# Transformer block on one core: Gelu's output and w2 split into f16 parts for the MLP's second product

## The reference

```
mod = swish(c) @ w_mod + b_mod                      # shifts, scales, gates
xn  = ln(x) * (1 + sc_msa) + sh_msa
q, k, v = heads(xn @ w_qkv + b_qkv);  q = ln(q, g_q);  k = ln(k, g_k)
x   = x + g_msa * (softmax(q k^T / 3) v @ w_proj + b_proj)
xn2 = ln(x) * (1 + sc_mlp) + sh_mlp
h   = gelu_tanh(xn2 @ w1 + b1)
out = x + g_mlp * (h @ w2 + b2)
```

## Time and profile before

| | us |
|---|---|
| median of 3 runs (190.43 to 191.2) | 190.98 |
| the profiled execution | 189.51 |
| its span | 187.7 |
| TensorE (PE) busy | 168.4 |
| VectorE (DVE) busy | 126.3 |
| ScalarE (ACT) busy | 107.4 |
| GpSimd (POOL) busy | 62.8 |

### The profile page before, as it was taken

One profiled execution on the slowest core, in us unless ns is written; L12 is line 12 of the kernel. 1 busy time (PEld: TensorE's weight loads), 2 busy tenths in 40 slices (PEclk: granted clock), 3 DMA queues, 4 the chain that ended last, 5 costly groups with the idle time before them and its releaser, 6 DMA issues.

```text
span 187.7 us, 4037 instructions
## 1 busy us (share of the span) xinstructions
PE 168.4 (90%) x1579; PEld 98.8 (53%) x1579; DVE 126.3 (67%) x317; ACT 107.4 (57%) x148; POOL 62.8 (33%) x81
## 2 busy tenths in 40 slices
PE   7999767549979999999999999999988899999983
PEld 2524324224354464654643654545545697969672
DVE  4359899475479698489788884985865676934111
ACT  3013040847898798788988988997929303060410
POOL 8203542458049555173190300205050325300000
PEclk9999999978999999999999999999999999999999
DMA  3747598300000000000000000000000000110101
GB/s 67 206 102 259 183 346 291 94 5 0 3 2 0 3 0 3 0 3 0 0 3 2 3 0 2 3 0 3 0 3 0 0 0 5 63 63 3 63 0 63
DMA packets 4536, 8.69 MB, mean 46 GB/s; under 512 B 821, under 2 KB 3071, under 8 KB 4406
## 3 DMA queue, kind: packets, MB, share of 16 engines
q1 hardware_dynamic: 4228, 8.41, 14.6%
q10 hardware_dynamic: 288, 0.01, 0.1%
HBM read 7.21 MB, written 1.21 MB: 45 GB/s over the span
## 4 chain that ended last, share of the span: by engine, by line
PE 65%; DVE 13%; ACT 8%; issue 5%; DMA 5%; POOL 2%; SPq 1%; DVEq 0%; ACTq 0%; POOLq 0%
PE ps_o L1139 17%; PE ps_o L1270 11%; PE ps_s L1124 9%; PE ps_s L1253 8%; ACT pTs L558 5%; PE ps_x L1055 5%; DMA lo_row<-in_lo_rows 5%; PE ps_x L1149 4%; PE ps_o L1167 3%; PE ps_x L1158 2%; PE ps_o L1048 2%; DVE bst L647 2%; PE ps_x L1167 1%; PE ps_o L1235 1%; PE ps_x L1235 1%
## 5 line engine op out<-in xcount | busy, mean ns | idle before, releaser
L558 ACT ACTIVATE pTs<-ps_s,escale 128x1024 f32<-128x1024 f32 x64 | 67.2, 1113 | 5.4 <-PE ps_s L1124 5.0
L1139 PE MATMUL ps_o<-pTs,v 128*32 128x256 f32 x512 | 37.0, 394 | 1.0 <-ACT pTs L558 1.0
L1124 PE MATMUL ps_s<-qT,kT 32*128 32x256 f16 x256 | 24.6, 275 | 3.5 <-ACT pTs L558 2.1
L618 ACT ACTIVATE late<-ps_s 120x512 f32<-120x512 f32 (+1 forms) x20 | 11.7, 599 | 24.5 <-PE ps_s L1253 24.5
L1023 PE MATMUL ps_x<-idle_z 128*128 128x512 f16 x75 | 19.5, 418 | 2.7 <-ACT raw L529 1.5
L1270 PE MATMUL ps_o<-w_sb,late 120*128 120x144 f32 (+1 forms) x160 | 20.7, 287 | 0.7 <-ACT late L618 0.7
L1270 PEld LDWEIGHTS ps_o<-w_sb,late 120*128 120x128 f32 (+1 forms) x160 | 19.9, 190 | 1.2 <-ACT late L618 1.2
L1139 PEld LDWEIGHTS ps_o<-pTs,v 128*32 128x32 f32 x512 | 12.6, 110 | 14.9 <-issue 9.1
L362 POOL TENSOR_SCALAR z<-xall,mv,rstd 128x144 f32<-128x144 f32 x14 | 16.6, 1191 | 8.8 <-DVE rstd L1331 5.1
L1253 PE MATMUL ps_s<-late,w1s 110*120 110x512 f16 (+1 forms) x80 | 18.5, 380 | 1.0 <-DVE late L891 0.8
L1124 PEld LDWEIGHTS ps_s<-qT,kT 32*128 32x128 f16 x256 | 7.3, 92 | 20.0 <-issue 11.9
(11 more groups left out here) (121 smaller groups left out, 260.1 us busy)
## 6 DMA issues: line engine op xcount, KB each, us to landing
mbc<-mod_rows SPq DMA_DIRECT2D x6, 432.0 KB, 8.2
late<-in_w SPq DMA_DIRECT2D x1, 990.0 KB
xall<-in_x SPq DMA_DIRECT2D x1, 864.0 KB, 5.2
out<-late SPq DMA_DIRECT2D x3, 288.0 KB, 2.2
z2s<-in_w_qkv SPq DMA_DIRECT2D x1, 742.5 KB
mbc<-mod_rows SPq DMA_DIRECT2D x2, 288.0 KB, 6.7
pTs<-in_w_mod SPq DMA_DIRECT2D x1, 486.0 KB
w_sb<-in_w SPq DMA_DIRECT2D x1, 337.5 KB
```

Of the source, the lines that this page charges most:

```text
L558: nc.scalar.activation(pT[u % NP].rearrange("p g n -> p (g n)"), ps_s[:, 2 * (u % 2):2 * (u % 2) + 2, :].rearrange("p a n -> p (a n)"), AC ...
L618: nc.scalar.activation(hT[k % 2][0:FW[f], f, :], ps_s[0:FW[f], (NF * k + f) % 4, :], ACT.Gelu_apprx_tanh, scale=UNSCALE).then_inc(gelued, 1)
L1124: mm = nc.tensor.matmul(ps_s[:, 2 * (u % 2) + a, half * N:(half + 1) * N], kT[par][rows, j, i * P:(i + 1) * P], qT[par][rows, j, :], start ...
L1139: mm = nc.tensor.matmul(ps_o[SLOT * g:SLOT * (g + 1), 1, (j % 2) * N:(j % 2 + 1) * N], v[par][:, i, h, :], pT[u % NP][:, g, :], start=(i = ...
```

## The change

w2 and the bias row b2 in it are scaled by 256 and split once: GpSimd writes the high f16 part `w2h`, VectorE the low part `w2l`, both within the attention iterations 1 and 2. Gelu now writes f32 into `h_f`, four chunk buffers inside `pTs`. ScalarE then copies it, times 4, into the high f16 part of `hT`; VectorE subtracts that from 4 times the f32 value and writes the low part (`low_part`). Each f32 product becomes three f16 products into the same PSUM tile: high with `w2h`, high with `w2l`, low with `w2h`. The output multiplication takes the factor 1/1024 in. `mlp_out` waits chunk by chunk for the low part on its first tile, in place of once for all Gelus, and Gelu m waits for low part m - 4. On VectorE's list the ten low parts of groups 0 and 1 are put between the other steps, `normalise(7)` goes ahead of `standardise2(2)` and `final(0)` ahead of `standardise2(3)`.

```diff
+        h_f = [pTs[0:FT, m // 2, m % 2 * 4 * P:(m % 2 + 1) * 4 * P] for m in range(4)]
...
+            pool.wait_ge(ld_w, 48)
+            pool.wait_ge(b2_row, 16)
+            nc.gpsimd.tensor_scalar(w2h[:], w2_sb[:], WS, None, ALU.mult).then_inc(w2_made, 1)
...
-                    nc.scalar.activation(hT[k % 2][0:FW[f], f, :], ps_s[0:FW[f], (NF * k + f) % 4, :],
+                    m = NF * k + f
+                    if m >= 4:
+                        act.wait_ge(h_low, m - 3)
+                    else:
+                        act.wait_ge(summed, B * U - 2)
+                    nc.scalar.activation(h_f[m % 4][0:FW[f]], ps_s[0:FW[f], m % 4, :],
                                          ACT.Gelu_apprx_tanh, scale=UNSCALE).then_inc(gelued, 1)
+                    act.wait_ge(gelued, m + 1)
+                    nc.scalar.activation(hT[k % 2][0:FW[f], 0, f, :], h_f[m % 4][0:FW[f]], ACT.Copy, scale=HS).then_inc(h_high, 1)
...
+                if n == 2:
+                    dve.wait_ge(w2_made, 1)
+                    nc.vector.scalar_tensor_tensor(w2l[:], w2_sb[:], WS, w2h[:], ALU.mult, ALU.subtract).then_inc(w2_made, 1)
...
+            def low_part(k, tiles):
+
+                for f in tiles:
+                    dve.wait_ge(h_high, NF * k + f + 1)
+                    if k >= 2:
+                        dve.wait_ge(y_pe, 2 * (k - 1))
+                    nc.vector.scalar_tensor_tensor(hT[k % 2][0:FW[f], 1, f, :], h_f[(NF * k + f) % 4][0:FW[f]], HS,
+                                                   hT[k % 2][0:FW[f], 0, f, :], ALU.mult, ALU.subtract).then_inc(h_low, 1)
...
             zT_half(1, 0)
+            low_part(0, range(0, 2))
             zT_half(1, 1)
+            low_part(0, range(2, 4))
+            normalise(B - 1)
+            low_part(0, range(4, NF))
             standardise2(2)
-            normalise(B - 1)
             channels(B - 1)
+            low_part(1, range(0, 1))
             stack2(2)
             projected(B - 1)
             residual(B - 1)
+            low_part(1, range(1, 2))
             aggregate(late_tiles)
             dve.wait_ge(root_pool, 2)
             roots(2, late_tiles)
+            final(0)
             standardise2(3)
-            final(0)
+            low_part(1, range(2, 3))
             zT_out(2)
+            low_part(1, range(3, NF))
             stack2(3)
             final(1)
+            low_part(2, range(0, NF))
             zT_out(3)
             final(2)
+            low_part(3, range(0, NF))
             final(3)
...
-                pe.wait_ge(gelued, NF * (k + 1))
                 if k < 2:
-                    pe.wait_ge(h_ones, k + 1)
-                    pe.wait_ge(b2_row, 16)
+                    pe.wait_ge(h_ones, 2 * (k + 1))
+                    pe.wait_ge(w2_made, 2)
...
                         for f in range(NF):
+                            if n == batches[0] and i == 0:
+                                pe.wait_ge(h_low, NF * k + f + 1)
                             r = FW[f] + (f == NF - 1)
-                            mm = nc.tensor.matmul(ps_o[:, n, i * H:(i + 1) * H], hT[k % 2][0:r, f, t * P:(t + 1) * P],
-                                                  w2_sb[0:r, f, :], start=(f == 0), stop=(f == NF - 1))
+                            nc.tensor.matmul(y, hT[k % 2][0:r, 0, f, tok], w2h[0:r, f, :], start=(f == 0), stop=False)
+                            nc.tensor.matmul(y, hT[k % 2][0:r, 0, f, tok], w2l[0:r, f, :], start=False, stop=False)
+                            mm = nc.tensor.matmul(y, hT[k % 2][0:r, 1, f, tok], w2h[0:r, f, :], start=False, stop=(f == NF - 1))
```

More of the change, by code:

```diff
@@ L48 @@
 UNSCALE = 1.0 / (XS * WS)
+HS = 2.0 ** 2
+YU = 1.0 / (HS * WS)
 SAFE_BOUND = 60.0
@@ L127, in build @@
         w2_sb = sb("w2_sb", [FT, NF, H])
+        w2h = sb("w2h", [FT, NF, H], F16)
+        w2l = sb("w2l", [FT, NF, H], F16)
         wp_sb = sb("wp_sb", [HT + 1, 2, H])
@@ L193, in build @@
         for i in range(2):
-            hT.append(late[0:FT, at:at + NF * T * P].rearrange("p (f n) -> p f n", f=NF))
+            hT.append(late[0:FT, at:at + NF * T * P].bitcast(F16).rearrange("p (a f n) -> p a f n", a=2, f=NF))
             at += NF * T * P
@@ L224, in build @@
         w1_made = sem("w1_made")
+        w2_made = sem("w2_made")
+        h_high = sem("h_high")
+        h_low = sem("h_low")
         set_dve = Steps(sem("set_dve"), "eps xs_one c_one c1 c2 c_s gp gneg gabs gmax gsafe ginv gbc "
@@ L633, in _ @@
             nc.vector.memset(o_ch[64:HT + 1], 1.0).then_inc(o_ones, 1)
-            nc.vector.memset(hT[0][FW[-1]:FW[-1] + 1, NF - 1, :], 1.0).then_inc(h_ones, 1)
+            nc.vector.memset(hT[0][FW[-1]:FW[-1] + 1, 0, NF - 1, :], HS).then_inc(h_ones, 1)
+            nc.vector.memset(hT[0][FW[-1]:FW[-1] + 1, 1, NF - 1, :], 0.0).then_inc(h_ones, 1)
             dve.wait_ge(set_act.sem, set_act.after(0, "c_e"))
@@ L971, in final @@
                     b = 2 * k + n
-                    nc.vector.tensor_tensor(yg[:, n, :].rearrange("p (i c) -> p i c", i=I),
-                                            ps_o[:, n, 0:I * H].rearrange("p (i c) -> p i c", i=I), mb(b, GM),
-                                            ALU.mult).then_inc(fin_dve.sem, 1)
+                    nc.vector.scalar_tensor_tensor(yg[:, n, :].rearrange("p (i c) -> p i c", i=I),
+                                                   ps_o[:, n, 0:I * H].rearrange("p (i c) -> p i c", i=I), YU, mb(b, GM),
+                                                   ALU.mult, ALU.mult).then_inc(fin_dve.sem, 1)
                     dve.wait_ge(fin_dve.sem, fin_dve.after(k, f"yg{n}"))
@@ L990, in _ @@
             dve.wait_ge(w1_made, 3)
-            nc.vector.memset(hT[1][FW[-1]:FW[-1] + 1, NF - 1, :], 1.0).then_inc(h_ones, 1)
+            nc.vector.memset(hT[1][FW[-1]:FW[-1] + 1, 0, NF - 1, :], HS).then_inc(h_ones, 1)
+            nc.vector.memset(hT[1][FW[-1]:FW[-1] + 1, 1, NF - 1, :], 0.0).then_inc(h_ones, 1)
             projected(B - 2)
@@ L1267, in mlp_out @@
                         t = n * I + i
+                        tok = slice(t * P, (t + 1) * P)
+                        y = ps_o[:, n, i * H:(i + 1) * H]
                         for f in range(NF):
+                            if n == batches[0] and i == 0:
+                                pe.wait_ge(h_low, NF * k + f + 1)
                             r = FW[f] + (f == NF - 1)
-                            mm = nc.tensor.matmul(ps_o[:, n, i * H:(i + 1) * H], hT[k % 2][0:r, f, t * P:(t + 1) * P],
-                                                  w2_sb[0:r, f, :], start=(f == 0), stop=(f == NF - 1))
+                            nc.tensor.matmul(y, hT[k % 2][0:r, 0, f, tok], w2h[0:r, f, :], start=(f == 0), stop=False)
+                            nc.tensor.matmul(y, hT[k % 2][0:r, 0, f, tok], w2l[0:r, f, :], start=False, stop=False)
+                            mm = nc.tensor.matmul(y, hT[k % 2][0:r, 1, f, tok], w2h[0:r, f, :], start=False, stop=(f == NF - 1))
                     mm.then_inc(y_pe, 1)
```

## The result

The change makes the kernel slower: 202.78 us median of 4 runs (202.47 to 203.47) against 191.09 for the kernel before. The ratio is 1.063 [1.059, 1.067]; on the 190.98 us of the forecast that is 203.0, 3.1 above the forecast of 199.9 and a hair past the upper end of its range (197.0 to 203.0). The profiled execution is the slowest of the four (203.47, span 201.7); that of before was 1.5 under its median (189.51, span 187.7). So the two traces are 14.0 us apart, the medians 11.7 to 12.

The account below looks back on a forecast made before the run. TensorE was taken to bound the kernel before, with VectorE's queue delaying it after the change. 6.8 + 0.5 + 0.5 = 7.8, plus 1.1 for the clock, on 190.98 gave 199.9 us; range 197.0 to 203.0.

Parts of the forecast that it names:

- VectorE's queue in groups 0 and 1: MLP: low parts and reordered steps make low part 9 late, so group 1's second product ends later: +6.8 us.
- groups 2 and 3: Last two groups: the chain Gelu, copy, low part behind the last chunk pays back TensorE's saving: +0.5 us each.
- clock, the fall in group 1: After TensorE's near-idle 158.4 to 167.8 us, following products run at the 1.2 GHz level: 1.1 us, at most 1.7.
- a second fall at the end: Rival, 0.10: the clock also falls in the wait before the last group's product: 1.5 us more, 201.4.
- No row here has the level fall while any matmul runs: Argument for the rival of the queue alone, without clock loss in group 1: 198.8, down to 198.0; chance 0.30.
- The written terms: Groups 0 and 1: delays ahead of standardise2(2), low part 5 meeting GpSimd (0.4), low part 6 (0.6), less 0.37 waiting.
- no idle time on VectorE from about 155: Sign of being right: VectorE never idle from about 155 to 168 us except waiting for the root.
- The range's high end: Whole kernel: low parts at 0.76, slower copies, full 1.7 of clock, half a second fall: +12, 203.0 us.
- Costed at nothing: w2h, w2l, two short memsets and the output multiply's other form: 0; w2h and w2l up to 1 us each uncovered.
- Weight loads do not set the pace of the f16 products: Denies a rival, 0.07: in the second products, f16 weight loads don't overlap, 1.7 us more in three groups: 205.0.
- VectorE keeps up: faster: Rival, 0.04: low part 9 is ready when TensorE reaches group 1's product, so most of 4.8 us stays saved: 189.6.

Follow-up runs that it names:

- 7: The kernel before, with 16 products that nothing reads put ahead of the wait in TensorE's idle stretch of 35.8 to 40.2 us: 188.28 us, ratio 0.989.
- 12: The change with filler products in TensorE's idle stretch in the middle and in its waits of groups 1 and 3: 197.28 us, ratio 1.039.
- 11: The change with 16 products that nothing reads in TensorE's idle stretch in the middle only: 199.35 us, ratio 1.048.
- Number 1: The change with zero products filling TensorE's waits in group 1 and in the last group, the middle not filled: 199.74 us, ratio 1.047.
- 8: The change with standardise2(2) back ahead of normalise(7) and standardise2(3) back ahead of final(0), low parts kept: 202.53 us, ratio 1.063.
- number 4: The kernel before with 18 zero matmuls behind TensorE's wait for raw, so they started only at 37.67 us: 191.14 us, ratio 0.997.

## Why the prediction was wrong, step by step

The sign and the mechanism of the queue were right, and the time was 3.1 us too low. By its own steps:

| step | forecast | measured | from |
|---|---|---|---|
| added operation on VectorE ahead of the last exponential | 0 | +0.4 | the pair 7 and 12 |
| VectorE's queue in groups 0 and 1 | +6.8 | +7.6 | the same pair |
| groups 2 and 3 | +0.5 each | +0.53, +0.54 | the same pair |
| clock, the fall in group 1 | +1.1 | +2.1 (1.8 to 2.0 in the traces) | numbers 11 and 12; the change against 12 |
| a second fall at the end, a longer low level in the middle | 0 | +0.5 to 0.8 | what is left of 11.7 to 12.0 |

The first four rows make 11.2. Of the 3.1 us that the forecast lacked, the clock in group 1 is 1.0, the queue 0.8, VectorE's added operation 0.4 and the last row the rest, which the runs don't divide. Number 1's 3.0 holds both falls at the end and whatever its middle happened to cost.

- **The step that failed is the clock, a term of the right kind that was sized too small.** "I take 1.1" was one fall, in group 1, discounted from 1.7 because part of the low level might pass before the work begins. It did not: the low level lay over the scattered products and 28 of the 48 that follow (to 174.1), and costs 9.39 - 7.63 = 1.8 us in the traces and 2.1 by numbers 11 and 12. The second fall, a rival with 0.10, happened in the profiled execution, whose last group takes 2.20 more instead of 0.54, so 1.7 us. Numbers 8 and 11 have the same waits there and no fall, so the argument against it, that 3.3 us of waiting is less than 4.48, decides it neither way. "No row here has the level fall while any matmul runs" was a misreading: 0.53 and not 0.50 from 40.20 on the earlier trace rows means that the level fell about 0.1 us after the transposes at 40.19 had begun.
- **The queue was right in kind, 0.8 short.** Standardise2(2) started 3.2 us later than before against the last exponential (3.0 forecast). GpSimd's modulate2(2) took 2.39 us and not 1.41 under low part 5, so 1.0 where 0.4 was written. By the last exponential final(0) starts 4.2 us later than standardise2(3) did before (21.20 against 17.00), where 3.4 was carried. The written terms (3.1, 0.4, 0.6, less 0.37) make 3.7; low part 6 was named and then left out of the sum. From final(0) to low part 9 the list took 7.1 us, as forecast (7.2). The pair at 167.90 met GpSimd and took 2.49 us (forecast: 0.6 and 1.9). The sign "no idle time on VectorE from about 155" did not come: it waited 2.78 us for GpSimd, to 157.39. The range's high end adds up to 11.6 and was written as 12.

```profile
153.49 2.39 POOL L483 TENSOR_TENSOR z2s<-z2s,mbc 128x576 f32<-128x576 f32 x1 [13.08 <-DVE z2s L891]
```

```profile
153.93 0.67 DVE L994 SCALAR_TENSOR_TENSOR late<-pTs,late 120x512 f16<-120x512 f32 x1
157.39 0.76 DVE L902 CAST zst<-z2s 128x1152 f16<-128x1152 f32 x1 [2.78 <-POOL z2s L487]
...
167.90 2.49 DVE L994 SCALAR_TENSOR_TENSOR late<-pTs,late 120x512 f16<-120x512 f32 x2
```

- **Costed at nothing, 0.4 off.** The second memset, on hT[1]'s row of the low part, stands on VectorE ahead of the multiply and the statistics for which ScalarE's logarithm waits, ahead of the last exponential: ScalarE waits 3.96 us there instead of 3.69. The other 0.17 of the 0.44 isn't assigned; all that w2h and w2l cost ahead of that point lies in it.
- **Weight loads do not set the pace of the f16 products.** The products start 62.6 ns apart, each with its own load, where the Trainium skill (TensorE: Matmul & The Clock Gate, Back-to-back issue gap) gives about 81 ns at 128 columns; the measurement decides. That rival falls.
- **The middle.** The traces differ by 1.88 us ahead of the last exponential, with the gap filled by 0.4. The other 1.4 goes with the low clock at the same idle stretch, which reaches to 43.6 us before and to about 48 in the change. Whether the change makes that low clock longer on average stays open: by the ratios the filler gave the kernel before 2.1 us (0.7 either way) and the change 2.9 (1.0 either way).
- **"VectorE keeps up: faster"**, 0.04, was wrong for this list and wanted more than VectorE's: with VectorE's list reordered the kernel is no faster than before (191.95), with both lists it came to 186.8. The rival was priced at 189.6; the groups' own chain could be covered as well.

## What to carry to other kernels

When a change puts work on an engine that has idle time but an in-order list, ask where in the list it will stand and who is behind it. Here 13.6 us of added work cost 13.4 us in one order, and in another the kernel with it is 2.6 us above the one without (191.95 against 189.36), and the waits it made cost the clock as well. Price each wait of several microseconds on TensorE twice, once as the wait and once as the products behind it at half speed. A stage whose operand comes from a chain over two engines gains from the next stage's work between its pieces; that is a change to TensorE's list, not to VectorE's.

## What the runs showed of the hardware

- **Scattered work did not keep the clock up.** In group 1 the level was 1.2 GHz from 163.9 to 174.1 us although TensorE had a burst of six products at 164.03 and of three at 166.84 and 168.65. In the last group, bursts of three products every 1.14 us were followed by a fall at 194.6 us, one microsecond into an unbroken run of products; the same bursts in numbers 8 and 11 were not (granted clock 1.00). Filler products in those waits held 2.4 GHz in both kernels that had them (numbers 1 and 12).
- **The cost of the same idle stretch varies from run to run.** In the kernel before, the profiled execution had the clock at 0.53 and 0.50 from 40.2 to 43.6 us; that of the change had 0.50 and 0.52 from 40 to 48. Of the kernel before with the late filler (number 4), five runs lie near 189.5 us at a mean clock of 0.997 to 0.999 and four near 191.2 at 0.989 to 0.991: one and the same program, 1.6 us apart. With the stretch filled in time four of six runs lie within 0.3 us of each other.
- **VectorE and GpSimd hold each other up, either way.** In the change GpSimd's operation at 153.49 took 2.39 us and low part 5 its usual 0.67. In the reordered kernel GpSimd's at 145.81 took its 1.41, and the low part begun 0.10 us behind it took 1.86. The Trainium skill (SBUF — State Buffer, SBUF: two separate sides) says that whichever starts first holds the shared pair of ports to its end. The second case agrees. By the records of the first GpSimd began 0.44 us ahead and was yet the one that waited: a copy out of PSUM, begun at 153.33, was still running on VectorE. What that copy had to do with it was not tried.
